# Records decoded, one-hots made and sums cleared in pieces inside the input phase of a graph network kernel

## The reference

```
Q = (h @ Wq.T + bq).reshape(-1, H, DH)
K = (h @ Wk.T + bk).reshape(-1, H, DH)
V = (h @ Wv.T + bv).reshape(-1, H, DH)
scores = einsum('ehd,egd->ehg', Q[src], K[tgt]) / sqrt(DH)
attn = softmax(scores, axis=-1)
msg = einsum('ehg,egd->ehd', attn, V[tgt]) + Ee[et]
return segment_sum(msg @ Wo.T + bo, src, num_segments=n_nodes)
```

## Time and profile before

| | |
|---|---|
| Median of 3 runs | 3940.0 us (3938.81 to 3954.16) |
| Profiled execution | 3954.87 us, its span 3953.1 us |
| PE busy | 3440.6 us (87%) |
| DVE busy | 2614.5 us (66%) |
| ACT busy | 2183.1 us (55%) |
| POOL busy | 2492.7 us (63%) |

### The profile page before, as it was taken

How to read it: one execution, slowest core, us unless ns; L and a number is a source line. 1 busy time by engine, 2 the same in 40 slices (tenths; PEclk the granted TensorE clock), 3 DMA queues, 4 the chain that set the end, 5 groups by cost and what they waited for, 6 DMA issues and landing times.

```text
span 3953.1 us, 102089 instructions
## 1 busy us (share of the span) xinstructions
PE 3440.6 (87%) x32589; PEld 2682.7 (68%) x32590; DVE 2614.5 (66%) x6732; ACT 2183.1 (55%) x6515; POOL 2492.7 (63%) x2501
## 2 busy tenths in 40 slices
PE   6887968888888898888889888888888888859998
PEld 3444657777777657777777755777777766659998
DVE  7887368887888646888788854888788884341111
ACT  4998855555555355555555535555555551224443
POOL 3776067777777427777777724777777772224444
PEclk9998989999999899999999989999999996769999
DMA  2000345555550035555554014555555203236664
GB/s 73 1 1 7 130 134 147 164 149 149 147 148 17 22 130 160 153 155 149 150 150 120 0 56 134 149 164 149 148 145 155 78 1 106 87 121 180 185 181 121
DMA packets 231294, 456.26 MB, mean 115 GB/s; under 512 B 90096, under 2 KB 134013, under 8 KB 222863
## 3 DMA queue, kind: packets, MB, share of 16 engines
q0 software_dynamic: 161376, 322.67, 30.9%
q1 hardware_dynamic: 69822, 132.43, 10.0%
HBM read 562.97 MB, written 47.19 MB: 154 GB/s over the span
## 4 chain that ended last, share of the span: by engine, by line
issue 27%; PE 27%; POOL 18%; DMA 9%; DVE 3%; POOLq 2%; ACT 1%; DVEq 0%; ACTq 0%
POOL arena L529 17%; DMA arena<-kv_d,gidx 8%; PE bank L1657 5%; PE bank L1669 5%; PE bank L1467 2%; PE bank L1501 2%; PE bank L1428 2%; PE bank L1444 2%; PE bank L1502 1%; PE bank L1457 1%; PE bank L1422 1%; PE bank L1549 1%; PE bank L1561 1%; POOLq L529 1%; POOL gidx L522 1%
## 5 line engine op out<-in xcount | busy, mean ns | idle before, releaser
L529 POOL DMA_INDIRECT arena<-kv_d,gidx x1764 | 1889.7, 1071 | 519.6 <-issue 481.2
L1227 ACT ACTIVATE kt_s<-bank 128x512 f32<-128x512 f32 x882 | 526.0, 596 | 823.9 <-PE bank L1444 821.2
L1457 PEld LDWEIGHTS bank<-qbd,kt_s 128*128 128x128 f32 x7056 | 937.8, 193 | 27.2 <-ACT kt_s L1227 3.4
L1444 PE MATMUL bank<-ident,arena 128*128 128x128 f32 x3528 | 683.5, 285 | 298.2 <-DMA arena<-kv_d,gidx 280.3
L1457 PE MATMUL bank<-qbd,kt_s 128*128 128x128 f32 x7056 | 932.8, 275 | 2.6 <-ACT kt_s L1227 2.6
L771 DVE TENSOR_REDUCE sc<-bank 128x32 f32<-128x512 f32 x882 | 610.2, 692 | 213.4 <-PE bank L1457 186.3
L1444 PEld LDWEIGHTS bank<-ident,arena 128*128 128x128 f32 x3528 | 403.2, 142 | 465.1 <-DMA arena<-kv_d,gidx 444.6
L797 DVE TENSOR_TENSOR att<-at_s,arena 128x512 f32<-128x512 f32 x882 | 612.9, 695 | 57.3 <-DVE at_s L790 36.5
L1467 PE MATMUL bank<-att,arena 128*64 128x64 f32 x14112 | 610.3, 229 | 19.7 <-DVE arena L814 19.7
L1467 PEld LDWEIGHTS bank<-att,arena 128*64 128x64 f32 x14112 | 488.5, 138 | 167.1 <-issue 150.6
L814 DVE TENSOR_TENSOR arena<-bank,arena 64x64 f32 x1764 | 393.5, 223 | 221.6 <-DVE arena L814 109.2
(11 more groups left out here) (239 smaller groups left out, 3969.6 us busy)
## 6 DMA issues: line engine op xcount, KB each, us to landing
arena<-in_pack SPq DMA_DIRECT2D x56, 1030.0 KB, 5.1
arena<-kv_d,gidx POOLq DMA_INDIRECT x1764
kv_d<-arena SPq DMA_DIRECT2D x50, 256.0 KB, 2.0
xin<-hid_d SPq DMA_DIRECT2D x75, 128.0 KB, 2.0
arena<-in_w SPq DMA_DIRECT2D x8, 1024.0 KB, 5.3
kv_d<-arena SPq DMA_DIRECT2D x5, 1280.0 KB, 5.3
hid_d<-arena SPq DMA_DIRECT2D x50, 128.0 KB, 2.0
rec_d<-arena POOLq DMA_INDIRECT x241
```

The costliest lines, as they stand in the source:

```text
L529: pool.indirect_dma_start(kv[:, t // UB, t % UB, :], None, kv_d, bass.IndirectOffsetOnAxis(gidx[:, h, t - h * HT:t - h * HT + 1], 0), boun ...
L1227: act.activation(kt_s[:, p % 2], bank[3 + p % 2][:, :].rearrange("p (u c n) -> p u c n", u=2, n=P), ACT.Copy).then_inc(S.kT_ready, 1)
L1444: ins = pe.transpose(bank[3 + p % 2][:, o:o + P], kv[:, t // UB, t % UB, c * P:(c + 1) * P], ident[:, :])
L1457: ins = mm(bk[:, o:o + P], kt_s[:, p % 2, u, c, :], qbd[:, p % 4, u, :], start=False, stop=(c == KC - 1), skip_group_check=True)
```

## The change

DVE's block of step 3 is taken apart and put into its loop of the input phase:

- decoding at step k = 2, behind a wait for the record load;
- the one-hots in 25 instructions of up to 24 columns (OH = 24, NOH = 25), one a step from k = 3 to 27;
- the lower half of `acc` in five memsets of 1280 elements at k = 3 to 7;
- the upper half in five `clear` of 1280 elements, four at k = 9, 14, 19, 24 behind `rows_stored` of their group, the fifth behind the loop, ahead of `edge_bias(0)`.

SP issues the record load ahead of the loop of stores and not behind it; it waits there for all 241 scatters. The counts that wait for `sums_zeroed` and `onehot_ready` follow the new numbers of instructions. Nothing else differs.

```diff
@@ -77,6 +77,8 @@
 ECP = -(-EC // CG) * CG
 PIECES = ((0, 96), (96, 192), (192, 296), (296, ECP))
 NWL, NWQ = 9, 4
+OH = TG * 3
+NOH = -(-ET // OH)
 RA = 4
 
 
@@ -387,6 +389,8 @@
             sp.wait_ge(S.wid_stored, 16)
             sp.dma_start(wid[:, :], wid_d[0:NTURN * TILES].rearrange("(a t) -> a t", a=1)).then_inc(S.wid_landed, 16)
 
+            sp.wait_ge(S.scattered, (NCH * KS + 1) * 16)
+            sp.dma_start(rec_in, rec_d.rearrange("(p t) x -> p (t x)", p=P)).then_inc(S.rec_landed, 16)
             for i in range(NG):
                 sp.wait_ge(S.xb_ready, (i + 1) * G)
                 sp.dma_start(group(xb_d, i), xall[:, i * G:(i + 1) * G, :]).then_inc(rows_stored[i], 16)
@@ -396,8 +400,6 @@
                 sp.dma_start(group(kv_d, i), kv0[:, i % 2]).then_inc(kvo_stored[i], 16)
             for j in range(G):
                 sp.wait_ge(h_stored[j], 32)
-            sp.wait_ge(S.scattered, (NCH * KS + 1) * 16)
-            sp.dma_start(rec_in, rec_d.rearrange("(p t) x -> p (t x)", p=P)).then_inc(S.rec_landed, 16)
 
             def load_h(l, n):
                 sp.dma_start(xin[:, n % G, :], hid_d[rows(n), :]).then_inc(rows_landed[n % G], 16)
@@ -561,7 +563,7 @@
                 for n in range(NT):
                     turn_sums(l, n)
                 pool.memset(acc, 0.0).then_inc(S.sums_zeroed, 1)
-                pool.wait_ge(S.sums_zeroed, l + 2)
+                pool.wait_ge(S.sums_zeroed, 2 * NG + 1 + l)
 
             def uf_phase(l):
                 pool.wait_ge(S.edges_all, l + 1)
@@ -763,7 +765,7 @@
                 dve.tensor_tensor(eewo[:, :], bank[0][0:TYPES, 0:D], bo4[:, :], ALU.add).then_inc(S.ee_ready, 1)
 
             def e_phase(l):
-                hold(dve, S.sums_zeroed, l + 1)
+                hold(dve, S.sums_zeroed, 2 * NG + l)
 
                 def best(q, at):
                     m = q % GP
@@ -968,6 +970,23 @@
                         dve.tensor_scalar(zb[:, n % G, :], x1[:, n % G, :], mv[:, 1, n % G, 0:1], rs2[:, n % G, 0:1],
                                           ALU.subtract, ALU.mult).then_inc(S.f_z, 1)
 
+            def clear(i):
+                n0 = o_x + i * G * D
+                dve.memset(arena[DH:P, n0:n0 + G * D], 0.0).then_inc(S.sums_zeroed, 1)
+
+            def decode():
+                dve.wait_ge(S.rec_landed, 16)
+                link(dve.tensor_tensor(rec_code, rec_in, pe_code, ALU.max))
+                dve.tensor_scalar(rec[:, :, 0], rec_code, 4, 4095, ALU.arith_shift_right, ALU.bitwise_and).then_inc(S.rec_ready, 1)
+                link(dve.tensor_scalar(rec[:, :, 1], rec_code, REAL + W - 1, None, ALU.bitwise_and))
+
+            def which(c):
+                t0, t1 = c * OH, min(ET, (c + 1) * OH)
+                dve.tensor_tensor(onehot[:, t0:t1, :],
+                                  iotas[:, :].unsqueeze(1).to_broadcast([P, t1 - t0, W]),
+                                  rec[:, t0:t1, 1].unsqueeze(2).to_broadcast([P, t1 - t0, W]),
+                                  ALU.is_equal).then_inc(S.onehot_ready, 1)
+
             def input_phase():
                 dve.wait_ge(S.std_ready, 1)
                 dve.reciprocal(rs0, sd0).then_inc(S.chain_in, 1)
@@ -995,27 +1014,26 @@
                             dve.wait_ge(h_stored[n // G - 2], 32)
                             dve.wait_ge(S.hT_done, G + n - 2 * G + 1)
                         dve.tensor_tensor(h0[:, n // G % 2, n % G, :], bank[n % 6][:, 0:D], b_in[:, :], ALU.add).then_inc(S.hout_ready, 1)
+                    if k == 2:
+                        decode()
+                    if 3 <= k < 3 + NOH:
+                        which(k - 3)
+                    if 3 <= k < 3 + NG:
+                        n0 = o_qa + (k - 3) * (o_x - o_qa) // NG
+                        dve.memset(arena[DH:P, n0:n0 + (o_x - o_qa) // NG], 0.0).then_inc(S.sums_zeroed, 1)
+                    i = (k - 9) // G
+                    if 9 <= k and (k - 9) % G == 0 and i < NG - 1:
+                        dve.wait_ge(rows_stored[i], 16)
+                        clear(i)
 
             bias(0)
             input_phase()
-            for j in range(G):
-                dve.wait_ge(rows_stored[j], 16)
+            dve.wait_ge(rows_stored[NG - 1], 16)
+            clear(NG - 1)
             edge_bias(0)
-            dve.memset(acc, 0.0).then_inc(S.sums_zeroed, 1)
-            dve.wait_ge(S.rec_landed, 16)
-            link(dve.tensor_tensor(rec_code, rec_in, pe_code, ALU.max))
-            dve.tensor_scalar(rec[:, :, 0], rec_code, 4, 4095, ALU.arith_shift_right, ALU.bitwise_and).then_inc(S.rec_ready, 1)
-            link(dve.tensor_scalar(rec[:, :, 1], rec_code, REAL + W - 1, None, ALU.bitwise_and))
-
-            for c in range(4):
-                n = ET // 4
-                t = rec[:, c * n:(c + 1) * n, 1]
-                dve.tensor_tensor(onehot[:, c * n:(c + 1) * n, :],
-                                  iotas[:, :].unsqueeze(1).to_broadcast([P, n, W]),
-                                  t.unsqueeze(2).to_broadcast([P, n, W]), ALU.is_equal).then_inc(S.onehot_ready, 1)
             wreg = [dve.alloc_register(f"wv{u}") for u in range(TILES)]
             dve.wait_ge(S.wid_landed, 16)
-            dve.wait_ge(S.onehot_ready, 4)
+            dve.wait_ge(S.onehot_ready, NOH)
             for l in range(L - 1):
                 e_phase(l)
                 uq_phase(l)
@@ -1613,7 +1631,7 @@
                              start=True, stop=True, skip_group_check=True)
                 ins.then_inc(S.cnt_done, 1)
             edge_bias(0)
-            pe.wait_ge(S.onehot_ready, 4)
+            pe.wait_ge(S.onehot_ready, NOH)
             for c in range(NOB):
                 if c >= 2:
                     pe.wait_ge(S.oht_copied, c - 1)
```

## The result

The changed kernel takes 3923.05 us (median; 3918.85 to 3932.09) against 3940.04 before: ratio 0.9947, 95% interval 0.9923 to 0.9970. The forecast was 3919.6, in a range of 3913 to 3934. Timed again in a later series it took 3921.57 against 3942.18: ratio 0.9947, interval 0.9935 to 0.9959. So the change gives 17 to 21 us where 20.4 were forecast.

The account below looks back on a forecast made before the run. POOL's indirect gathers were taken to bound the edge phase. POOL's earlier start, 517.4 to 497.0 including a 2.7 us shift, gains 20.4 us; off the median 3940.0 that gives 3919.6, range 3913 to 3934.

Parts of the forecast that it names:

- POOL is the pace: Edge phase: it ends when POOL has issued its last gather, so moving POOL's first gathers counts if PE is ready.
- POOL's 20.4 us: Start of first edge phase: POOL's gather stream begins at 497.0 instead of 517.4 us, a gain of 20.4 us.
- The additions cost 0: Input phase: one-hots and clearing, 1.55 us in a tile with both, fit DVE's 2.4 us idle per tile; 0 us.
- Rival C: Input phase: the additions do not hide and DVE is late for PE in every tile; 3935 to 3942 us, chance 0.06.
- The stall: Start of input phase: DVE's wait for the record load shifts the phase by 2.7 us, bounds 0 and 6.8.
- The clock: Start of input phase: PE's idle 2.7 us loses no clock; if it fell, about 2.3 us, at most 3.
- First gather and keys: Start of first edge phase: POOL's first gather at 497.0 us, PE's keys at 508.3 instead of 531.00, gaining 22.7.
- counting back of three slow gathers: First edge phase before the change: from the fourth gather at 521.33, 3.90 us back, the stream began as if at 517.4.
- The slow first gathers: First edge phase: three gathers of 2.2 to 2.4 us, slowed by DVE's L1013; if merely first, 3.2 us come back.
- rival B: Stall dearer: load takes 5.9 us, clock falls or first gathers stay slow; gain 13 to 18, 3922 to 3927, chance 0.34.
- A: Whole kernel: the forecast with its small terms at their better values; 3916 to 3923 us, chance 0.52.
- E: Decode wait: DVE and PE stand until all 241 scatters land, a backlog making the kernel slower; 3950 us, chance 0.03.

Follow-up runs that it names:

- e6b: Changed kernel with five memsets on POOL between its wait for the cnt products and its first index copy; 3936.93 us in one run.
- e2c: Changed kernel with one-hots, memset and clearing put back behind the input phase, record load and decoding left early; 3942.4 us, ratio 0.9996 to the kernel before.
- e4: Changed kernel with every one-hot piece made twice, run on a slower chip only; 4513.56 us, ratio 0.9957 to the kernel before.
- e5: Changed kernel with 45 extra products on PE ahead of layer 0's first key transposes; 3942.5 us in one run.
- a2: The changed kernel itself once more, nothing altered; 3921.57 us, ratio 0.9947 to the kernel before.
- e1b: Changed kernel with decoding at step k = 6 instead of 2 and one-hots in 19 larger pieces behind it; 3922.81 us, ratio 0.9943 to the kernel before.
- e2: Kernel before with only record load and decoding moved early, memset and one-hots left behind the input phase; ratios 0.9973 and 0.9966 on two slower chips.

## Why the prediction was right, point by point

- **POOL is the pace.** Right in the changed kernel (e6b: a first gather 11.2 us later gives a first update 11.6 later, while keys are 4.2 later), with the limit of 15 to 16 us for PE. "POOL gains less and paces" held, since PE's gain came with it. Had PE's block not moved, POOL's 20.4 us would have been worth next to nothing (e2c). The text treated PE's side as merely sufficient; it is the half without which there is no gain.
- **The additions cost 0.** Right. Estimated at 0.48 and 1.07 us, measured 0.55 and 1.12; DVE's wait was left at 0.49 and 1.94 us where 0.9 to 1.9 was written. I had left out the 0.32 us of issue ahead of a memset. Rival C is refuted, by PE's 77.00 of 77.00, by tiles of the same length and by e4.
- **The stall.** The term of 2.7 us measured 3.6 (PE's L1604 against x0T), with 3.91 us of PE's idleness, and 1.10 us of idleness in the second execution. Its parts erred in both directions: the scatters were done sooner (SP issues the load 2.04 us after the last scatter starts, where 3.2 was taken) and the load took longer, 2.9 to 5.0 us in six traces (2.5 taken). The bounds 0 to 6.8 held.
- **The clock.** Taken at no loss. That was the weakest step: in the changed kernel's first trace, in e2c and in e5 the clock fell 2.0 to 2.1 us into PE's idle stretch, so a stretch of 2.7 us as forecast would have lost it too by these traces. It cost some 2.5 us in the profiled execution; in a2 PE stood only 1.10 us and kept it. The shift of the input phase was 6.2 there (108.3 - 102.1) and 1.4 in a2, around the forecast of 2.7 and, with the loss, 5.0. The rule of the Trainium skill ("TensorE: Matmul & The Clock Gate", "Why this matters for your kernels"), that idle gaps return the array to half rate, agrees with the first trace (2.1 us of idleness and then 0.50) and doesn't apply in the second (1.10 us, and 1.00).
- **First gather and keys.** 498.3 and 509.2 instead of 497.0 and 508.3, in an execution that began 2.3 us sooner. Against x0T the gather gained 134.9 - 118.1 = 16.8 us (131.2 made 134.9 by the forecast's own counting back of three slow gathers) and the keys 19.5, where 20.4 and 22.7 were forecast; the missing 3.5 are the shift that was too small. In a2 it is 23.8 and 26.9: the shift was 1.3 us smaller than forecast, and the clock held 2.2 us longer in the count products, which no term allowed for.
- **How good the number is.** The first median's gain of 17.0 us and the 16.8 that the stream's start gained in the profiled execution fit each other, both 3.5 below the forecast, and the shift explains them. That the second gain, 20.6, hits the forecast's 20.4 is chance: in that execution the stream gained 23.8.
- **The slow first gathers.** They go with L1013 and not with being first, as taken. Had they stayed, 3.2 us of the gain would have been lost.
- **Rivals.** In the profiled execution rival B happened in part (stall 0.9 above its term, clock 2.5); of the medians 3923.05 lies just above A and in the lower part of B, 3921.57 in A. E falls: the scatters had no backlog.

What stays open: why the gathers of one layer take up to 4.6 us more in one execution than in another, and stages behind the first layer 7 to 12 us, which hides what late decoding wins, and why e5 lost 15 us more than its first layer shows.

## What to carry to other kernels

Where an engine waits for another in every tile, its idle time can carry setup work from a serial block behind the loop; count its wait per tile, take the instruction with its issue time, and look whether the wait is left above zero in the tile that has all additions. When two engines start a stage through a ring of buffers, moving one earlier is worth at most what is left of the ring's slack: move both, and check the distance between their first instructions. A wait put into a pipeline's filling costs more than its length if it lets the clock fall; a few steps later there was none left (e1b), though the whole time did not show the difference.

## What the runs showed of the hardware

- PE's clock fell after 2.1 us of idleness in one execution, after 2.1 (387.2 to 389.3) in e2c_stall_only and after 2.0 in e5_pe_late, and stayed up over 1.10 us in a2 and 0.36 in e6b. It rose again 5.0, 5.9 and 4.8 us after work resumed.
- Being busy doesn't keep the clock up by itself. In all eight traces of the faster chips it fell to 0.50 during the count products (48 rows, 4 columns of weights, 200 moving columns), 2.5 to 5.2 us after the first of them, with PE busy 1.00 of each microsecond. Eight of them start in a microsecond before it falls and 5 after.
- A gather's length on POOL beside DVE's TENSOR_TENSOR with two SBUF inputs depends on the length of that instruction: 2.17 to 2.35 us beside pieces of 2.56 us, 1.10 beside pieces of 0.47, 1.00 beside nothing or a memset. This looks like POOL waiting out the instruction that runs, not sharing with it. The Trainium skill, page "Trainium Architecture — The Big Picture", section "What this means for kernel authors", says of the port that both use "it's an exclusive lock (not a bandwidth split)"; these numbers agree. So many short pieces hurt a neighbour less than few long ones.
- The same program took 15 and 17% longer on two chips, with a mean granted clock of 0.89 to 0.90 in their traces instead of 0.95 to 0.96, and with gaps named "remote" and "issue" of up to 11.6 us on ACT. The kernel of e2 gained 12 to 16 us there and nothing on another chip; POOL's waits show another pace, but why the early gathers pay there was not tested.
